# Products with the values of two groups in one block, with four buffers of exponentials

## The reference, cut to what matters

```python
qkv = jnp.einsum('oc,bct->bot', qkv_w, h) + qkv_b[:, None]
ch = C // NUM_HEADS
qkv = qkv.reshape(B * NUM_HEADS, 3 * ch, T)
q, k, v = (qkv[:, :ch], qkv[:, ch:2 * ch], qkv[:, 2 * ch:])
scale = 1.0 / jnp.sqrt(jnp.sqrt(jnp.asarray(ch, q.dtype)))
w = jnp.einsum('bct,bcs->bts', q * scale, k * scale)
w = jax.nn.softmax(w.astype(jnp.float32), axis=-1).astype(q.dtype)
a = jnp.einsum('bts,bcs->bct', w, v).reshape(B, C, T)
out = jnp.einsum('oc,bct->bot', proj_w, a) + proj_b[:, None]
return (xr + out).reshape(x.shape)
```

## Time and profile before

| what | value |
|---|---|
| median of three runs | 2296.9 |
| lowest, highest | 2295.36, 2297.52 |
| profiled execution, its span | 2295.6 |
| TensorE busy | 2201.2 |
| VectorE busy | 1815.8 |
| ScalarE busy | 1719.9 |
| GpSimd busy | 520.6 |
| granted clock of TensorE, share of full speed | 0.994 |

### The profile page before, as it was taken

How to read it: one execution, slowest core, us unless ns; L and a number is a source line. 1 busy time by engine, 2 the same in 40 slices (tenths; PEclk the granted TensorE clock), 3 DMA queues, 4 the chain that set the end, 5 groups by cost and what they waited for, 6 DMA issues and landing times. The chain is left out here.

```text
span 2295.6 us, 34006 instructions
## 1 busy us (share of the span) xinstructions
PE 2201.2 (96%) x11776; PEld 972.2 (42%) x11776; DVE 1815.8 (79%) x3176; ACT 1719.9 (75%) x3107; POOL 520.6 (23%) x689
## 2 busy tenths in 40 slices
PE   3999999999999999999999999999989999999998
PEld 1223232323333232333333232333326888888887
DVE  2878888888888878888888888888837777777776
ACT  1467677777877777776767777776777888888887
POOL 3113030202213030311203020211113333333331
PEclk9999999999999999999999999999999999999999
DMA  6053351606244261616345160615112112121111
GB/s 82 7 70 53 58 78 35 104 22 91 41 69 66 45 90 36 95 27 84 50 61 76 36 103 22 94 37 75 26 31 72 53 48 66 36 65 57 42 53 49
DMA packets 81647, 132.31 MB, mean 58 GB/s; under 512 B 17632, under 2 KB 50528, under 8 KB 81504
## 3 DMA queue, kind: packets, MB, share of 16 engines
q1 hardware_dynamic: 78240, 129.70, 32.5%
q10 hardware_dynamic: 3264, 0.79, 0.2%
HBM read 53.12 MB, written 17.83 MB: 31 GB/s over the span
## 5 line engine op out<-in xcount | busy, mean ns | idle before, releaser
L447 DVE TENSOR_REDUCE h_half_nmax<-h_s_ps 128x1 f32<-128x512 f32 x2048 | 1285.8, 684 | 270.2 <-PE h_s_ps L682 263.0
L598 ACT ACTIVATE h_probs<-h_st_ps 128x512 f32<-128x512 f32 x2048 | 1103.7, 600 | 388.2 <-PE h_st_ps L819 382.2
L682 PE MATMUL h_s_ps<-h_krep,h_qrep 96*128 96x512 bf16 x2048 | 795.7, 389 | 22.4 <-SPq L232 20.8
L819 PE MATMUL h_st_ps<-h_qrep,h_krep 99*128 99x512 bf16 x2048 | 779.9, 382 | 35.1 <-DMA h_qrep<-h_mrow 24.3
L674 PE MATMUL h_pv<-h_probs,h_vT 128*32 128x512 f32 x4096 | 548.1, 607 | 0.9 <-ACT h_probs L598 0.7
L682 PEld LDWEIGHTS h_s_ps<-h_krep,h_qrep 96*128 96x128 bf16 x2048 | 200.0, 98 | 677.3 <-DVE h_half_nmax L447 503.0
L819 PEld LDWEIGHTS h_st_ps<-h_qrep,h_krep 99*128 99x128 bf16 x2048 | 201.7, 99 | 230.6 <-DMA h_qrep<-h_mrow 36.4
L347 POOL TENSOR_SCALAR h_nparts<-h_nmax 128x16 bf16<-128x16 f32 x64 | 16.4, 256 | 956.6 <-DVE h_nmax L455 956.6
L1334 PE MATMUL o_s<-o_k,o_q 128*128 128x512 f32 x768 | 225.7, 430 | 7.4 <-DVE o_q L1155 5.8
L1334 PE MATMUL o_pv<-o_pT,o_vT 128*128 128x512 f32 x768 | 208.1, 406 | 0.8 <-ACTq L1261 0.8
L1149 DVE TENSOR_TENSOR o_pT<-o_t,o_pT 128x512 fp32r<-128x512 f32 x256 | 164.5, 684 | 43.8 <-ACT o_pT L1286 41.4
(11 more groups left out here) (116 smaller groups left out, 1380.1 us busy)
## 6 DMA issues: line engine op xcount, KB each, us to landing
h_krep<-h_kp SPq DMA_DIRECT2D x96, 256.0 KB, 8.7
h_qrep<-h_qp SPq DMA_DIRECT2D x192, 128.0 KB, 9.5
x_res<-out_dram SPq DMA_DIRECT2D x24, 512.0 KB, 3.7
num<-av SPq DMA_DIRECT2D x128, 64.0 KB
rrep<-rden_dram SPq DMA_DIRECT2D x16, 512.0 KB
out_dram<-o_y SPq DMA_DIRECT2D x16, 512.0 KB
out_dram<-h_y SPq DMA_DIRECT2D x15, 512.0 KB, 2.6
o_x_in<-out_dram SPq DMA_DIRECT2D x15, 512.0 KB, 3.5
```

The source lines that it names most:

```text
L447: reduce = nc.vector.tensor_reduce(half_nmax[:, c, unit:unit + 1], s_ps[bank(2 * n + c)][:, :], AX.X, ALU.max, negate=True)
L598: nc.scalar.activation(probs[g % 2][:, j, :], st_ps[bank(n)][:, :], ACT.Exp, scale=1.0 / CH ** 0.5).then_inc(exp_done, 1)
L682: nc.tensor.matmul(s_ps[bank(n)][:, :], qrep[par][0:KS, th, head, tile * P:(tile + 1) * P], krep[par][0:KS, head, c * HALF:(c + 1) * HALF] ...
L819: nc.tensor.matmul(st_ps[bank(n)][:, :], krep[par][0:KM, head, st * P:(st + 1) * P], qrep[par][0:KM, th, head, :], start=True, stop=True). ...
```

## The change

The block of two groups stands together. In each even group k, behind the third column product, come the products of group k-2 and then those of group k-1; odd groups have none. Since the exponentials of a group are now read up to two groups later, `probs` has four buffers in place of two, and the starting value and the waits of `pv_done` go from 2 to 4. At the very end the last two groups' products follow each other.

```diff
+    PROBS = 4
...
-        probs = [sb(f"probs{i}", [P, QUAD, HALF]) for i in range(2)]
+        probs = [sb(f"probs{i}", [P, QUAD, HALF]) for i in range(PROBS)]
...
-                act.wait_ge(pv_done, n + 2)
+                act.wait_ge(pv_done, n + PROBS)
...
-                            nc.scalar.activation(probs[g % 2][:, j, :], st_ps[bank(n)][:, :], ACT.Exp,
+                            nc.scalar.activation(probs[g % PROBS][:, j, :], st_ps[bank(n)][:, :], ACT.Exp,
...
-            act.wait_ge(pv_done, 2)
+            act.wait_ge(pv_done, PROBS)
...
-                                               probs[k % 2][:, j, :], start=(k % TILES == 0),
+                                               probs[k % PROBS][:, j, :], start=(k % TILES == 0),
...
-            pe.sem_inc(pv_done, 2)
+            pe.sem_inc(pv_done, PROBS)
...
-                            if j == 2 and not (first and n < QUAD):
+                            if j == 2 and k % 2 == 0 and not (first and n < QUAD):
+                                products(k - 2)
                                 products(k - 1)
...
             pe.wait_ge(exp_done, QUAD * (4 * GROUPS + 1))
+            group_products(3, GROUPS - 2).then_inc(pv_done, 1)
             group_products(3, GROUPS - 1).then_inc(pv_done, 1)
```

## The result

| | before | changed |
|---|---|---|
| median of four runs | 2297.2 | 2372.9 |
| lowest, highest | 2295.4, 2298.9 | 2371.1, 2378.0 |
| profiled span | 2295.6 | 2376.0 |
| granted clock of TensorE, share of full speed | 0.994 | 0.987 |

The ratio is 1.0336, with a 95% interval of 1.0323 to 1.0349: slower by 76. The forecast was 2368, range 2322 to 2403. The profiled execution took 2378.0, 1.9 of it outside its span, and is the slowest of the four; the other three had a granted clock of 0.990 to 0.991.

What follows compares the result with a forecast made beforehand. TensorE sets the pace, narrowly, with reductions slower than row products in a burst. 15 x 4.40 = 66.0, plus 1.5 + 0.6 and 2.4, gave +70.5 on 2295.6, 2366; with 1.3 for the runs' median, 2368 us, range 2322 to 2403.

Steps and rivals of the forecast that it cites:

- The sign and the mechanism: Eight-head part: slower by 70.5 us, since row products at 0.44 outrun reductions at 0.60 with three banks; chance 0.66.
- The walk: Timing of each pair of groups, product by product: a plain odd-step pair takes 6.00 us against 5.69.
- The gain: Block switches in TensorE: each costs about 0.18 us in and out, half disappear; a two-group block takes 1.90, not 2.00.
- my lower bound of 1.88: Shortest expected two-group block in us, its second group's inner passes at 0.44: 0.46 + 2 x 0.44 + 0.54.
- The side work: Even steps: coefficients, normalisations and projection evacuation delay reductions or exponentials; +0.79 us in groups 0-2, +0.64 in 2-6.
- The small statistics of group 11: Odd step, groups 10 to 12: about 0.45 us on VectorE pushes the fifth reduction back, 5.69 to 6.45, +0.76.
- The DMA of the maxima: Even step, groups 14 to 0: 1.91 us of waiting absorbs TensorE's 0.8 longer way; cost 0, bounds -0.2 and +0.8.
- ScalarE's buffers: ScalarE's new waits for a free buffer of exponentials cost nothing, the block asked for being over at least a group.
- TensorE's busy share: Sign expected in the changed kernel's timeline: a drop of about three points from 96%.
- the faster one: Rival: banks don't bind, so each of 256 pairs gains 0.18 us, about 2254 us; chance 0.06.
- Nothing saved inside the block: Rival: the double block takes 2.00 us, 256 x 0.10 = 25 more, 2393 us; chance 0.12.
- Side work caught up: Rival: VectorE and ScalarE catch up side work during the block, half the loss, 33 us, 2330 us; chance 0.13.

Runs made afterwards that it cites:

- the two swapped products: Changed kernel with a row product on both sides of each double block, against a run with the double block one product later (2365.0): 2353.3 us.
- the changed kernel with one of the ten half-clock stretches left: Changed kernel plus products that nobody reads, four at each odd step's start and five behind the last group of each body: 2362.0 us.

## Why the prediction was right, point by point

- **The sign and the mechanism**: eight row products in a row outrun three banks that come back at VectorE's pace. Shown by the weight loads' waits, by the shorter reductions (5.45 a pair) and by the two swapped products (5.79). The walk had only the eighth row product wait for long (0.5) and the fifth to seventh less; in the trace the sixth to eighth wait 0.48 each. The sum is the same, since the last one ends the chain.
- **The gain**: the drain at the switches was priced right and comes out a little larger. The double block takes 1.86, not 1.90, and lies under my lower bound of 1.88: the inner passes start 0.45, 0.43 and 0.43 apart. That is 0.04 in each bank-bound pair, some 9 in all on the fast side.
- **The side work** of the even steps was right within 0.06 a pair. The small statistics of group 11 were mis-sized: 0.46 instead of 0.76 for that pair. The 0.45 that I took held 0.17 in which VectorE waited for TensorE; a distance between starts isn't a price where a wait stands in it.
- **The DMA of the maxima**, priced at 0, cost 0.17 at the median. It hid 0.8 of TensorE's own way, as the walk said; without the wait those appear.
- **ScalarE's buffers**, priced at 0, cost 0.
- **A sign that failed**: TensorE's busy share was to drop by about three points and dropped by 1.6 (95.9% to 94.3%), since a part of its waits counts as busy.
- **What the forecast lacked**: the granted clock. Its terms alone came to 70.5, and the changed kernel with one of the ten half-clock stretches left took 2362.0, 65 over before. By the medians of the table a pair of steps costs 3.74 more, not 4.40; group 11 (0.30) and the block (0.04 in each of seven pairs) are most of that. The clock adds 11. (2296.9 + 70.5 is 2367.4; the forecast says 2368.) Two misses of opposite sign made 2368 look closer to 2372.9 than the sum deserved.
- **Rivals**: the faster one fell with the first weight load wait of 0.48. Nothing saved inside the block: no. Side work caught up: no, except in part in group 11; that rival put a pair of steps at 2.05.

## What to carry to other kernels

Joining work to save a switch also joins what stood between: count how many results the consumers must take in the longer burst, against the banks that hold them and the rate at which they come back, before counting the switches. Where the consumer is slower than the producer inside a burst, short blocks in between are its time to catch up, even if the producer's engine is 96% busy. And look at the repeated wait that bounds a whole step before the pattern inside it: holding six DMAs back until a small urgent one was issued brought 1.35%, while every reordering of the blocks cost time or gained none.

## What the runs showed that I had not expected

- TensorE's clock falls after idle times that it had survived in another order. At the starts of bodies TensorE's starts stood 1.8 apart in the changed kernel, and it fell to half clock in six of seven, in all seven with the DMAs held; in the kernel before they stood 1.4 apart and it never fell. At the other step starts with a wait they stood 1.7 to 2.5 apart in the kernel before (3.3 at the first), and it fell at the first and at one more; in the changed one they stood 1.1 to 2.3 apart (3.1 at the first), and it fell at the first and at three more. What else counts besides the length of the idle time these runs don't settle. Five fillers behind each body kept the clock, and 10 us (2349.5 to 2339.5).
- Inside column-tiled blocks the second group's pieces follow at 0.43 a pass, with no loss between groups (starts 899.52, 899.97, 900.40, 900.83, and the next row product at 901.38); the whole price of the arrangement is on its way in (0.09) and out (0.11 to 0.12).
- A DMA of 12 KB on ScalarE's queue had its last packet 7.0 to 7.9 us after its issue when twelve of 128 KB had been issued on SyncE's queue before it, and 1.7 us after it when none of them was under way or six were held back.
